# Combining the experts of a graph layer: VectorE alone, or TensorE with diagonal gate matrices for three of four experts

## The reference, cut to what matters

```python
scores = _layernorm(agg, ln_gamma, ln_beta).reshape(M, HEADS, NUM_EXPERTS).mean(1)
topk_s, topk_i = jax.lax.top_k(scores, TOP_K)
w = jax.nn.softmax(topk_s, axis=-1)
out = jnp.zeros_like(x)
for ei in range(NUM_EXPERTS):
    g = jnp.where(topk_i == ei, w, 0.0).sum(-1)
    hh = jax.nn.gelu(x @ W1[ei] + b1[ei], approximate=False)
    out = out + g[..., None] * (hh @ W2[ei] + b2[ei])
...
x = x + ffn(x)
```

## Time and profile before

| | |
|---|---|
| median of 3 executions | 3715.11 us (3713.55 to 3723.78) |
| the profiled execution, its own time | 3719.9 us |
| its span, first to last instruction | 3718.3 us |
| last stage, combination part | 3613.5 to 3718.3 us of the span |
| busy over the whole span | PE 67%, DVE 48%, POOL 49%, ACT 17% |

### The profile page before, as it was taken

The page is one execution under the profiler, slowest core; times in us unless marked ns, Lnnn a source line. Parts: engine busy times, 40 slices in busy tenths (PEclk is TensorE's granted clock), DMA queues, the critical chain, the costliest instruction groups (busy, mean ns, idle before and its releaser), DMA issues. The chain is left out here.

```text
span 3718.3 us, 36268 instructions
## 1 busy us (share of the span) xinstructions
PE 2473.0 (67%) x11702; PEld 1930.6 (52%) x11702; DVE 1768.4 (48%) x3555; ACT 629.0 (17%) x837; POOL 1815.5 (49%) x1886
## 2 busy tenths in 40 slices
PE   2788888888888687788888875999999800000000
PEld 2677777777777556455665553666666600000000
DVE  8555555555555344898799990010000000001887
ACT  1111111111111132122222221112112100000100
POOL 0666666666666200132231314777777777774310
PEclk8777877777777799899999987999999955555555
DMA  6544443344333322111010104222232211114315
GB/s 206 181 110 111 113 110 108 109 110 113 108 110 110 124 77 89 63 40 46 23 46 32 37 22 81 66 66 62 60 73 55 61 16 15 15 17 177 98 53 199
DMA packets 178583, 307.54 MB, mean 83 GB/s; under 512 B 41427, under 2 KB 119890, under 8 KB 176726
## 3 DMA queue, kind: packets, MB, share of 16 engines
q0 software_dynamic: 70816, 136.49, 15.4%
q1 hardware_dynamic: 79002, 132.29, 11.0%
q10 hardware_dynamic: 28700, 37.99, 3.1%
HBM read 228.82 MB, written 77.81 MB: 82 GB/s over the span
## 5 line engine op out<-in xcount | busy, mean ns | idle before, releaser
L396 POOL DMA_INDIRECT xg<-xn_dram,gidx x784 | 741.2, 945 | 417.7 <-issue 221.4
L1892 POOL DMA_INDIRECT er<-row_dram,gi x832 | 787.3, 946 | 279.3 <-issue 237.7
L420 PE MATMUL ps_e<-we,eaT 65*128 65x256 f32 x1568 | 476.1, 456 | 182.7 <-DVE msg L544 175.9
L439 PEld LDWEIGHTS ps_a<-inwin,msg 128*128 128x128 f32 x3136 | 539.5, 259 | 21.7 <-ACT msg L463 3.2
L439 PE MATMUL ps_a<-inwin,msg 128*128 128x128 f32 x3136 | 536.1, 344 | 2.8 <-ACT msg L463 2.8
L420 PEld LDWEIGHTS ps_e<-we,eaT 65*128 65x128 f32 x1568 | 340.5, 228 | 253.0 <-DVE msg L544 193.5
L463 ACT ACTIVATE msg<-msg 128x1024 f32<-128x1024 f32 x196 | 207.1, 1057 | 982.8 <-DVE msg L544 943.2
L2013 DVE TENSOR_TENSOR eo<-ps_en,eb_r 128x1024 f32<-128x1024 f32 (+1 forms) x52 | 60.5, 1163 | 657.4 <-PE ps_en L1964 657.4
L1955 PE MATMUL ps_em<-xT,ew 128*128 128x512 f32 (+1 forms) x832 | 345.0, 570 | 41.1 <-DMA xT<-x3T_dram 41.1
L1346 POOL TENSOR_SCALAR hg<-hg,mv,rs 128x256 f32<-128x256 f32 x49 | 97.2, 1992 | 555.3 <-DVE rs L1116 555.3
L1964 PE MATMUL ps_en<-ew,hid 128*128 128x256 f32 x1568 | 344.8, 379 | 0.0
(11 more groups left out here) (283 smaller groups left out, 2697.3 us busy)
## 6 DMA issues: line engine op xcount, KB each, us to landing
eaT<-in_eaT SPq DMA_DIRECT2D x98, 256.0 KB, 3.8
eo_dram<-eo SPq DMA_DIRECT2D x48, 512.0 KB, 3.0
eo<-eo_dram SPq DMA_DIRECT2D x12, 2048.0 KB, 11.3
er<-row_dram,gi POOLq DMA_INDIRECT x832, 2.4
xg<-xn_dram,gidx POOLq DMA_INDIRECT x784, 2.8
xm<-xm_dram SPq DMA_DIRECT2D x24, 512.0 KB, 4.0
erow<-none ACTq DMA_DIRECT2D x1, 10240.0 KB, 35.9
erow<-er POOLq DMA_DIRECT2D x52, 160.0 KB, 2.1
```

The source lines that it names most:

```text
L396: pool.indirect_dma_start(xg[:, q, b, :], None, M["xn_dram"], bass.IndirectOffsetOnAxis(ap=gidx[:, q, b:b + 1], axis=0)).then_inc(s_g[q][b ...
L420: t = pe.matmul(ps_e[h][:, b * D:(b + 1) * D], eaT[:, q, h * HB + b, :], we[:, :], start=True, stop=True)
L439: t = pe.matmul(ps_a[:, q, c * P:(c + 1) * P], msg[:, q, b, c * P:(c + 1) * P], inwin[:, q, b, :], start=False, stop=False, skip_group_che ...
L1892: pool.indirect_dma_start(er[:, r, b, :], None, M["row_dram"], bass.IndirectOffsetOnAxis(ap=gi[:, r, b:b + 1], axis=0)).then_inc(s_get[r], 16)
```

## The change

Only `attend_and_combine` changes, and in it only the combination.

- EB goes from 6 to 5 buffers for `eo`. The room goes to `dgm`, [128, 4, 3, 128]. Two PSUM tiles `ps_c`, [128, 4, 256], are added.
- ScalarE makes, for each tile and for the experts 1, 2 and 3, a diagonal matrix: the identity times the row's gate (`spread`, an ACTIVATE Copy with a scale of one number per partition).
- TensorE multiplies each diagonal with the expert's rows and sums the three products in PSUM: three float32 matmuls of 128x128 by 128x256 per tile, 12 in a group.
- VectorE does residual + g0\*e0 (`first_expert`, four instructions in a group) and adds the sum from PSUM in one instruction (`combine`, 128x1024).
- All loops of the combination are written out. VectorE's order is `first_expert(0)`, `first_expert(1)`, `combine(0)`, `first_expert(2)`, `combine(1)`, and so on; ScalarE's is `spread(0)`, `spread(1)`, store 0, `spread(2)`, store 1, and so on.

```diff
-    EB = NG // 2
+    EB = 5
...
+        dgm = sb("dgm5", [P, G, NE - 1, P])
+        ps_c = [ctx.enter_context(nc.psum_tensor(f"ps_c5{b}", [P, G, D], F32)) for b in range(2)]
...
+        def groups():
+            return [(i, G if i < NG else 1) for i in range(NG + 1)]
...
-                def load(j, b, T):
-
-                    sp.wait_ge(s_out[b], j)
-                    sp.dma_start(eo[:, b, 0:T, :, :], M["eo_dram"][:, bass.ds(j * (EB * G) + b * G, T), :, :]).then_inc(s_eo[b], 16)
-
-                over_groups(sp, load, EB)
+                for i, T in groups():
+                    if i >= EB:
+                        sp.wait_ge(s_out[i % EB], i // EB)
+                    sp.dma_start(eo[:, i % EB, 0:T, :, :], M["eo_dram"][:, i * G:i * G + T, :, :]).then_inc(s_eo[i % EB], 16)
...
+                def spread(i, T):
+
+                    for t in range(T):
+                        n = i * G + t
+                        if n >= G:
+                            act.wait_ge(s_dr2, n - G + 1)
+                        for x in range(1, NE):
+                            y = nc.scalar.activation(dgm[:, t, x - 1, :], M["ident"][:, :], ACT.Copy, scale=g[:, n, x:x + 1])
+                        y.then_inc(s_dg, 1)
...
+                act.wait_ge(s_gd, 1)
+                for i, T in groups():
+                    spread(i, T)
+                    if i:
+                        put(i - 1, G)
+                put(NG, 1)
...
+            @block.tensor
+            def _(pe):
+                for i, T in groups():
+                    pe.wait_ge(s_eo[i % EB], i // EB * 16 + 16)
+                    if i >= 2:
+                        pe.wait_ge(s_out[(i - 2) % EB], (i - 2) // EB + 1)
+                    for t in range(T):
+                        pe.wait_ge(s_dg, i * G + t + 1)
+                        for x in range(1, NE):
+                            y = pe.matmul(ps_c[i % 2][:, t, :], dgm[:, t, x - 1, :], eo[:, i % EB, t, x, :], start=(x == 1), stop=(x == NE - 1))
+                        y.then_inc(s_dr2, 1)
+                    pe.wait_ge(s_dr2, i * G + T)
+                    pe.sem_inc(s_pc, 1)
...
-                def combine(j, b, T):
-                    i = j * EB + b
-                    s = Steps(dve, s_dc, i, (NE - 1) * G + G - 1)
-                    dve.wait_ge(s_eo[b], j * 16 + 16)
-
-                    dve.wait_ge(s_st[b % 2], j * (16 * EB // 2) + 16 * (b // 2))
-                    for x in range(NE):
-                        for t in range(T):
-                            n = i * G + t
-                            before = acc[:, b % 2, t, :] if x else M["xn"][:, n, :]
-                            y = nc.vector.scalar_tensor_tensor(acc[:, b % 2, t, :], eo[:, b, t, x, :], g[:, n, x:x + 1], before, ALU.mult, ALU.add)
...
+                dve.sem_inc(s_gd, 1)
+
+                def first_expert(i, T):
+
+                    dve.wait_ge(s_eo[i % EB], i // EB * 16 + 16)
+                    if i >= 2:
+                        dve.wait_ge(s_st[i % 2], 16 * (i // 2))
+                    for t in range(T):
+                        n = i * G + t
+                        z.done(nc.vector.scalar_tensor_tensor(acc[:, i % 2, t, :], eo[:, i % EB, t, 0, :], g[:, n, 0:1], M["xn"][:, n, :], ALU.mult, ALU.add))
+
+                def combine(i, T):
+
+                    dve.wait_ge(s_pc, i + 1)
+                    dve.wait_ge(s_dc, i * G + T)
+                    nc.vector.tensor_tensor(acc[:, i % 2, 0:T, :], ps_c[i % 2][:, 0:T, :], acc[:, i % 2, 0:T, :], ALU.add).then_inc(s_out[i % EB], 1)
+
+                z = Chain(dve, s_dc)
+                for i, T in groups():
+                    first_expert(i, T)
+                    if i:
+                        combine(i - 1, G)
+                combine(NG, 1)
```

More of the change, by code:

```diff
@@ L2078, in attend_and_combine @@
         s_ge = sem("s_ge5")
+        s_gd = sem("s_gd5")
         s_out = [sem(f"s_out5{b}") for b in range(EB)]
@@ L2081, in attend_and_combine @@
         s_go = sem("s_go5")
+        s_dg = sem("s_dg5")
+        s_dr2 = sem("s_dr25")
+        s_pc = sem("s_pc5")
+        def groups():
+            return [(i, G if i < NG else 1) for i in range(NG + 1)]
         def rounds(eng):
@@ L2109, in _, with put @@
                 nc.scalar.activation(g[:, :, :], g[:, :, :], ACT.Exp).then_inc(s_ge, 1)
-                def put(j, b, T):
-                    i = j * EB + b
-                    act.wait_ge(s_out[b], j + 1)
-                    rows, p = (T * P, P) if T == G else (LAST, LAST)
-                    act.dma_start(out[bass.ds(i * (G * P), rows), :].rearrange("(t p) d -> p t d", p=p), acc[0:p, b % 2, 0:T, :]).then_inc(s_st[b % 2], 16)
-                over_groups(act, put, EB)
+                def spread(i, T):
[6 more added lines that the diff above has]
+                        y.then_inc(s_dg, 1)
+                def put(i, T):
+                    act.wait_ge(s_out[i % EB], i // EB + 1)
+                    rows, p = (T * P, P) if T == G else (LAST, LAST)
+                    act.dma_start(out[i * (G * P):i * (G * P) + rows, :].rearrange("(t p) d -> p t d", p=p), acc[0:p, i % 2, 0:T, :]).then_inc(s_st[i % 2], 16)
+                act.wait_ge(s_gd, 1)
[4 more added lines that the diff above has]
+                put(NG, 1)
                 act.wait_ge(s_st[0], 16 * (NG // 2 + 1))
```

## The result

The changed kernel takes 3742.39 us (median of 5, 3741.42 to 3746.86) against 3715.11 us before: ratio 1.007, 95% interval [1.0055, 1.0085]. It is slower by some 27 us, although it takes more than half of VectorE's work in the combination away. The forecast was 3742 us in a range of 3729 to 3758. The time before is also a median of 5 here (3713.55 to 3723.78); it is the same as that of the first three.

A forecast was written before the change was run, and what follows sets the result against it. VectorE bounds the kernel's combination; afterwards serial store waits would: combine(0) at 3623.4, seven periods of 12.7, 7.7, two of 6.3, 5.1, 0.6 and 4.9 us give span 3743.3 against 3718.3, +25 us; forecast 3742 us, range 3729 to 3758.

The forecast's parts named there:

- The mechanism: Combination: VectorE waits for the store just issued, so stores go one after another, seven beside a full load; +25 us.
- TensorE becomes the bound: Rival, combination: the clock stays at 0.50, a group takes 10.6 us on TensorE; +39 us, 3754 us; chance 0.08.
- The start: From gates done at 3613.5 to the end of combine(0) at 3623.4, bounds -2.3 and +3.6 us.
- The first burst: TensorE's matmuls of the first group, starting at half clock: 7.3 us, between 5.3 and 10.6, exposed only at the start.
- L: Landing time of a store in the combination: 9.2 us beside a full load, bounds 8.0 and 11.4.
- the period: Time per group in the combination, a store's landing plus 3.5 us: 12.7 us seven times, in place of 7.05 plus waits.
- Store 7: Store beside the last load of 512 KB: lands in 2.8 + 1.4 = 4.2 us, period 7.7 us.
- The end: Stores 8 to 10 land in 2.8 us: periods 6.3 twice, then 5.1, last tile 0.6, last store 4.9 us.
- The last tile: The one tile left after combine(11) at the end of the combination: 0.6 us.
- Five buffers: Five eo buffers for six, fewer bytes loaded at the stage's start: no gain, 0.2 us at best.
- Written-out loops: Combination without loop issue steps, some 0.1 us a group gone: counted as nothing, bounds -1 and +3 us.
- two bases: Times before to add +25 us to: profiled execution 3719.9 us gives 3745, median 3715.1 us gives 3740; 3742 put.

The follow-up runs named there:

- e1: Changed kernel with VectorE's combine(i) directly behind first_expert(i): 3715.2 us, ratio 0.9983 to the kernel before.
- e3: Changed kernel, order kept, with a third acc buffer in memory the attention no longer uses: 3712.4 us, ratio 0.9984 to the kernel before.
- e5: Changed kernel with loads 5 to 12 cut to one tile of one expert (128 KB for 2048 KB): 3698.4 us, one run.
- e4: Changed kernel with load i + 5 also waiting for the landing of store i: 3719.8 us, ratio 1.0013 to the kernel before.
- e8: Changed kernel with one diagonal and one matmul a tile, experts 2 and 3 left out: 3737.0 us, one run.
- e6: Kernel before with five eo buffers and its combination loops written out, nothing on TensorE: 3714.9 us, ratio 1.0.
- e9: Changed kernel with each load after the gates cut into four by expert (1 KB pieces): 4664.1 us against 4669.7 for the kernel before beside it.
- e7: Changed kernel with e1's VectorE order, six eo buffers and three acc buffers: 3695.0 us, ratio 0.9941 to the kernel before.
- e2: Changed kernel with e1's VectorE order and six eo buffers: 3704.4 us, ratio 0.9969 to the kernel before.
- e12: e7 with all loads cut into four by expert (1 KB pieces): 3684.4 us, ratio 0.9913 to the kernel before.

## Why the prediction was right

**The mechanism.** Right, and shown from four sides: take the wait away by order (e1) or by a buffer (e3), or take the load from beside the store (e5), and 27, 30 and 44 us go; delay the load behind the store's start (e4), and 23 go. One sentence of the prediction is too wide: no compute of VectorE runs beside a store, but TensorE's and ScalarE's does, as the burst at 3649.69 shows. The rival "TensorE becomes the bound" is out: e8 saves 7 us of the part, not 36.

**The start.** Forecast 3623.4 for the end of `combine(0)`; measured 3623.62, with gates 0.7 us earlier. The first burst was 8.21 us, not 7.3; three diagonals took 0.99 us, not 1.1. The burst was mis-sized by the clock: I read it as full from about 3 us on, where the earlier trace rows have 0.50 until 2288 and 0.88 in the three us after, a rise about 3.7 us into the burst, and in the changed kernel it rose about 5.6 us in (0.65 in the stretch from 3619 to 3620, 1.00 after). The first bursts of the runs here with three diagonals a tile took 6.9 to 8.3 us.

**L and the period.** L was taken as 9.2 us; the seven landings in the chain have a mean of 9.3 (8.96 to 10.05). The period was 85.87 / 7 = 12.3 us (store issues 3623.65 to 3709.52), forecast 12.7. What lies between landing and issue is 2.9 us and not 3.5: VectorE starts 0.1 us after the landing and not 0.3, the store is issued 0.03 us after the addition and not 0.2, and the addition starts before the last of the four instructions is through (3634.95 against 3633.36 + 1.67). Seven times 0.4 is 3 us too many.

**Store 7.** The mis-sized term with the other sign: 4.2 us forecast, 5.73 measured. A quarter of 6.3 is 1.6 and not the 1.4 of my sum, so 4.4; a quarter of the load costs more than a quarter of its delay even so.

**The end.** Periods of 5.7 us for 6.3, again 0.6 less each. From the last VectorE instruction to the end of the span there are 6.4 us (3734.4 to 3740.8), not 4.9. The last store is issued 0.4 us behind the one before it (3734.11 and 3734.53), where it was 1.8 us (3711.58 and 3713.39); that this is the reason wasn't tested. The last tile itself came sooner than forecast. The sum: span 3740.8 against 3743.3, with errors of 1 to 3 us in both directions.

**Parts costed at nothing.** Five buffers: e6 shows no loss, and the attention began at 3425.1 against 3426.0, with a gather of 15.83 us. Written-out loops: I had 0.1 us a group as gain, a figure that no row showed; e6 shows 0.34 us a group on VectorE in the old form. It did not matter in the changed kernel, where VectorE waits anyway.

**The median.** I put the forecast between two bases 4.8 us apart; the profiled execution of the changed kernel was itself the median one, so nothing in it tells which base was better. The spans of the two profiled executions differ by 22.5 us where I had 25, and the medians by 27.3. That 3742 was hit to less than 1 us is luck; that it is some 25 us slower isn't.

**The rule of the Trainium skill** cited in the prediction (DMA: Bandwidth & Descriptors, Rules for kernel authors: issue early, wait late) agrees with the runs: e3 lets the wait for a store come a group later (and moves acc to other memory), e1 does it by order alone, and they give 30 and 27 us.

**Where my own model failed** is in the expectations of e1 and e3: 3703 us was said, 3715 and 3712 came. The failed step is "7.8 us a group once two stores are in flight", that is engine time in order of issue. The runs showed 14.4 to 17.5 us in the chain of e1, and 10.9 to 17.8 in that of e3, for a store that meets a second load. The Trainium skill, in DMA: Bandwidth & Descriptors, Queues, rings and completion order, states that each DMA engine goes round its queues packet by packet. e9 agrees in direction: with 1 KB pieces on both sides the store is through in 5.2 to 6.1 us, with 16 KB pieces against its 1 KB in 9.0 to 10.1. It is not the whole account, since equal turns alone would have given 4.3, and the later issue of the load's parts stands beside it untested.

## What to carry to other kernels

When work is taken from the busiest engine, look for what that work was hiding: here 7 us of VectorE per group covered most of a store of 9 us, and an order that waits for the store just issued laid it open in full. The time of a store is a property of what is in flight beside it: 2.8 us alone, 9.3 beside one large load, 10.9 to 20.9 in the chains of e1, e3 and e7, where a second load comes before it has landed (in e7 a third too). TensorE's help pays only as far as the stores get out of the way: nothing that clears the noise by order alone (e1), 6 us with a third acc buffer (e3), 12 and 21 us with six buffers for eo and the new order (e2, e7). Cutting the loads gave the old kernel 18 us by itself, and both together 34. A third acc buffer in the old kernel wasn't tried; its waits for stores are 11.8 us in all.

## What the runs showed of the hardware that I had not expected

- Cutting the loads into 1 KB pieces costs rate, and still paid. At the start of the stage, with the 16 DMA engines full of loads and before the gather, the kernel before moves 431 GB/s and e12 359 (its rows, the last two figures the DMA share and GB/s):

```profile
3401.00:3404.00 3.00, 0.00 (x0) 0.00 (x0) 1.60 (x5) 0.00 (x0) 0.24 (x2) 0.50 1.01 431
```

```profile
3398.00:3401.00 3.00, 0.00 (x0) 0.00 (x0) 1.76 (x5) 0.00 (x0) 0.41 (x2) 0.50 1.09 359
```

- The granted clock fell back from 1.00 to 0.50 once a burst of TensorE was over, though the gaps are only 3.6 to 5.9 us: ahead of the burst at 3661.83, but in the one at 3649.69 only after some 0.7 us of it (1.00 in the stretch from 3649 to 3650, 0.71 in the next). In the burst at 3661.83 it stayed at 0.50 until after 3667:

```profile
3661.00:3664.00 3.00, 2.17 (x5) 1.84 (x6) 0.00 (x0) 3.00 (x12) 0.00 (x0) 0.50 1.00 337
3664.00:3667.00 3.00, 3.00 (x8) 2.36 (x8) 0.00 (x0) 0.31 (x2) 0.00 (x0) 0.50 1.00 372
3667.00:3670.00 3.00, 3.00 (x13) 2.24 (x11) 0.68 (x2) 0.00 (x0) 0.00 (x0) 0.92 0.46 165
```

  A burst of 24 records took 7.1 to 8.3 us that way and 5.42 us where bursts follow within 1.5 us. After the first burst it cost nothing in the changed kernel, since the store is longer; in e12 the first burst is the only slow one.
- An added wait made a kernel faster by 23 us (e4), because it moved a load out of the way of a store.
